# Splitting a block scatter in two and reordering every engine's queue in a recurrent attention kernel

## The chip, the cores and the metric
One core of one Trainium2 chip. The time is the device time of one execution in microseconds, as the median of three runs. The engines are PE (TensorE), DVE (VectorE), ACT (ScalarE), POOL (GpSimd) and SP (SyncE, which here only issues transfers). Each runs its own list of instructions in order and waits on semaphores for the others.

## The reference
Two layers on 1024 tokens (2 sequences of 512) of width 256. Layer 0 is causal softmax attention with 16 heads of 16 and a mixture of 8 experts of which each token uses 2. Layer 1 is a gated delta-rule recurrence, followed by 2 shared and 16 routed experts (2 per token). The recurrence is most of the time; per key head (16 of width 128, two value heads each) and token it does

```
Sk    = einsum("bhi,bhipj->bhpj", k_t, state)
delta = (v_t - Sk) * b_t
state = state * d_t + einsum("bhi,bhpj->bhipj", k_t, delta)
o     = einsum("bhi,bhipj->bhpj", q_t, state)
```

after a causal convolution of four taps over q, k and v, and before an RMS norm, a gate silu(z) and an output projection.

## The kernel before
The recurrence is cut into chunks of 128 tokens: 16 heads times 4 chunks give 64 units `u` (head h = u // 4, for both sequences and both value heads at once). Inside a unit the token-by-token rule becomes a triangular system. Its steps carry short names, by which the planner knows them:

- `row`, `dec`: the decay row is fetched (tile RC), POOL adds the bias and masks it, ACT takes the exponential.
- `gram`, `pt`: PE forms K K^T and Q K^T, DVE scales them into M and PTE. `pl`, `pm`, `py`: POOL splits M and adds the identity.
- `a` and `b`, once for each level: the ladder that inverts the unit triangular matrix by doubling. `a` is a PE product with a DVE copy (ZF, ZL), `b` a PE product with an ACT copy (XYLM). `r`, `c` finish the inverse (DVE tiles R and W).
- `KS`, `U`, `so`: the state step, which each unit hands to the next. `sq`, `on`, `ot`, `os`, `ol`, `y`, `yl`: norm (ACT, POOL), transpose (PE, with the gate on DVE), splitting (POOL) and output projection (PE).

Per head there are also the projections `ck`, `cq`, `cv` (PE), each with three convolution taps on DVE (`ck1` to `cv3`, line L2148), `kn` (norm of the keys), `Vt`, `Zt`. From head 2 on the first levels of the inverse are done for a whole head at once on DVE and POOL: LM is parked in DRAM (`ls`), its 16x16 diagonal blocks are gathered (`dg`, 8 transfers), inverted (`iv1`, `p8`, `iv2`, `q8`, `iv3`), copied by ACT (`xc`, tile XY) and scattered back into the parked array by `sx`: for each of 8 blocks and each of 2 matrices one transfer of 8 KB, 16 in a row on SP. Then `ld` loads each unit's matrices (XYLM).

Layer 1 also needs the routing of its 16 experts: `cnt` (PE, then DVE), `own`, `tiles` and `hits` are arithmetic on DVE alone (L1832 to L1891), `slot` a small product; after that POOL issues indirect transfers, `sw` for expert weights (L2745) and `sr` for token rows (L2729), and `sT`, `su`, `sd` run the tiles in 8 groups.

All of this is one list of parts with an engine, an assumed cost and predecessors. `Plan.arrange` places them one after another: of the ready parts it takes the one with the smallest begin time (plus an offset from the table LATER), in steps of 0.0517 us, and breaks ties by rank plus an offset from the table RANK. What comes out is the fixed order of each engine's instructions and the PSUM bank of each product. The engines then run those orders with semaphores. `cum` is the product that ends the preparation of the decays; `pre(4)` is the DVE step behind it. In what follows a part is named with its indices, such as `so(0,1)`, the state step of unit 0, second sequence.

Of the kernel before, what the change touches and what calls it, by code (L numbers as in the profile page):

```python
# [78 lines left out]
RANK = {  # L79
    "KS": {"ACT": 15.02}, "KS:first": {"ACT": 149.13, "DVE": 1181.68, "PE": 1010.25},  # L80
    "KS:last": {"ACT": -222, "DVE": -206.26, "PE": 190.34}, "U": {"ACT": -18.46, "PE": -931.18},
    "U:first": {"ACT": -151.06, "PE": 608.87}, "U:last": {"ACT": 335.37, "PE": -335.84}, "Vt": {"ACT": 90.31},
    "Vt:first": {"ACT": 3712.37, "PE": 1204.71}, "Zt": {"ACT": -129.73}, "Zt:first": {"ACT": 4.87},
    "a": {"DVE": -1349.82}, "a:first": {"DVE": 740.41, "PE": -888.94}, "a:last": {"DVE": 24.87, "PE": -779.69},
    "am:0": {"POOL": -60.05}, "am:1": {"POOL": 376.57}, "b": {"ACT": 1157.23},
    "b:first": {"ACT": -993.02, "PE": -2311.64}, "b:last": {"ACT": -395.1, "PE": -102.16},
    "c": {"DVE": -4239.84, "PE": -1258.51}, "c:first": {"DVE": -25.7, "PE": -55.9},
    "c:last": {"DVE": 213.97, "PE": -5.57}, "cb": {"DMA": 10.36, "DVE": -81.97, "POOL": -375.65},
    "cc": {"POOL": -343.13}, "ck": {"ACT": 922.98}, "ck1": {"DVE": 973.5}, "ck1:first": {"DVE": -591.14},
    "ck2": {"DVE": 768.74}, "ck2:first": {"DVE": 155.35}, "ck3": {"DVE": 253.77}, "ck3:first": {"DVE": 284.76},  # L90
    "ck:first": {"ACT": -349.27, "PE": -22.49}, "cnt": {"DVE": 580.25, "PE": -336.59}, "cq": {"ACT": -31.68},
# [10 lines left out]
    "fWV": {"POOL": 260.31, "SP": -44.28}, "fin": {"DVE": -134.8, "SP": -83.9}, "fld": {"SP": -358.28},
    "fs": {"ACT": 250.33}, "fst": {"SP": 132.24}, "fup": {"POOL": 169.77, "SP": -539.82},
    "fx": {"POOL": -199.89, "SP": -573.4}, "g0": {"ACT": 80.6}, "gg": {"DVE": -115.68, "PE": -29.2},
    "gram": {"DVE": 41.18, "PE": -508.06}, "gram:first": {"DVE": -141.6, "PE": -416.39},
    "gram:last": {"DVE": 154.44, "PE": -407.02}, "gt": {"ACT": 337.25, "PE": -330.13}, "hits": {"DVE": -209.58},
    "iv1": {"DVE": -424.93}, "iv2": {"DVE": -224.76}, "iv3": {"DVE": -443.76}, "kb": {"POOL": 171.24},
    "kb:first": {"POOL": 14.23}, "kn": {"ACT": 1374.77, "POOL": 134.84},
    "kn:first": {"ACT": 275.87, "PE": -156.91, "POOL": -308.37}, "kns": {"ACT": -780.5},
    "kns:first": {"ACT": -329.63}, "ld": {"DMA": -180.19, "SP": -410.02}, "ld:last": {"DMA": 45.92, "SP": 283.5},  # L110
    "ln1": {"ACT": -20.84, "DVE": 222.58, "PE": -88.46}, "ls": {"DMA": 81.69, "SP": -20.91},
    "ls:last": {"DMA": 56.89, "SP": 366.03}, "max": {"SP": 2.19}, "mk:0": {"POOL": 433.31}, "mk:1": {"POOL": 219.74},
    "nr2": {"DVE": -44.87}, "nrm": {"POOL": -113.07}, "oc:0": {"ACT": 189.5}, "oc:1": {"ACT": -379.67},
    "ol": {"POOL": -32.95}, "ol:first": {"POOL": -31.41}, "ol:last": {"POOL": 774.22}, "on": {"ACT": -904.27},
    "on:last": {"ACT": -566.16}, "op": {"DVE": 286.87, "PE": -1756.01}, "os": {"POOL": -177.43},
    "os:first": {"POOL": 81.33}, "os:last": {"POOL": -38.41}, "ot": {"DVE": -204.1, "PE": -586.61},
    "ot:first": {"DVE": -24.55, "PE": -145.69}, "ot:last": {"DVE": 322.85, "PE": -452.77},
    "ov:1": {"DVE": -366.86, "PE": 232.57}, "own": {"DVE": -429.99}, "p1:0": {"DVE": -68.36, "PE": -121.26},
    "p1:1": {"DVE": 27.26}, "p8": {"POOL": -213.19}, "pd": {"DMA": 325.19, "SP": -895.26},
    "pd:first": {"DMA": 175.96, "SP": 517}, "pd:last": {"DMA": 313.5, "SP": -493.56},  # L120
    "pf": {"DVE": 172.9, "SP": 243.4}, "pl": {"POOL": 6.37}, "pl:first": {"POOL": 15.59}, "pl:last": {"POOL": -36.33},
    "pm": {"POOL": 68.09}, "pm:first": {"POOL": 634.35}, "pm:last": {"POOL": 639.07},
    "pre": {"ACT": -830.11, "DVE": 94.48}, "ps": {"DMA": -177.84, "SP": 3.21},
    "ps:first": {"DMA": -267.15, "SP": -317.62}, "ps:last": {"DMA": 20.34, "SP": 735.5}, "pt:last": {"DVE": -311.51},
    "pv:0": {"PE": 8.46}, "pv:1": {"PE": -666.95}, "py": {"POOL": 1261.98}, "py:first": {"POOL": 206.17},
    "q8": {"POOL": 6.96}, "r": {"DVE": -581.63}, "r:first": {"DVE": -65.75, "PE": -1765.17},
    "r:last": {"DVE": -57.39, "PE": -1050.4}, "rb:0": {"SP": -298.18}, "rc:0": {"DVE": 1012.4},
    "rc:1": {"DVE": -121.62}, "rd:0": {"SP": 78.63}, "rd:1": {"SP": 210.21}, "row": {"DMA": -531.58},
    "row:first": {"DMA": -85.8, "SP": -250.3}, "row:last": {"DMA": 241.31, "SP": -1186.17}, "rt1": {"DVE": 298.72},
    "sT": {"ACT": -139.9, "PE": 3.29}, "sc:0": {"ACT": -400.63, "PE": 0.38}, "sc:1": {"ACT": 450.62, "PE": -125.1},  # L130
    "sd": {"DVE": 1296.02}, "slot": {"DVE": -98.48, "PE": -539.68}, "so": {"DVE": -153.94, "PE": -273.42},
    "so:first": {"DVE": 578.75, "PE": -1724.17}, "so:last": {"DVE": 0.93, "PE": -188.84}, "spg": {"POOL": -19.8},
    "sq": {"ACT": 298.13, "POOL": -483.87}, "sq:first": {"ACT": 126.75}, "sq:last": {"ACT": 593.63},
    "sr": {"POOL": -624.67}, "ss": {"SP": -5.07}, "stack": {"SP": -387.27}, "su": {"ACT": -324.78},
    "sw": {"DMA": 73.95, "POOL": 13.31}, "sx": {"DMA": -333.8, "SP": 100.24}, "tiles": {"DVE": 6.35},
    "tn": {"DVE": 265.94, "PE": -10.92}, "tn0": {"DVE": -15.3}, "top": {"ACT": -537.19, "DVE": 25.86},
# [4 lines left out]
    "yl:first": {"DVE": 1177.21, "PE": -193.29}, "yl:last": {"DVE": 19.32, "PE": 30.9},  # L141
}


LATER = {
    "KS": {"ACT": 0.21}, "KS:first": {"ACT": 0.05, "DVE": 0.02}, "KS:last": {"ACT": 0.16, "DVE": 0.43},
    "U:first": {"ACT": 0.06}, "U:last": {"PE": 0.25}, "Vt": {"ACT": 0.38}, "Vt:first": {"ACT": 0.21},
    "am:0": {"POOL": 0.76}, "am:1": {"POOL": 0.36}, "b:last": {"ACT": 0.25}, "c:last": {"PE": 0.14},
    "cb": {"DMA": 1.91, "DVE": 0.84}, "ck1:first": {"DVE": 0.07}, "ck3": {"DVE": 0.03}, "ck:first": {"ACT": 0.7},
# [2790 lines left out]
```

## Time and profile before
| | us |
|---|---|
| median of 3 runs | 1229.77 (1229.45 to 1232.14) |
| the profiled execution | 1230.72 |
| its span | 1228.9 |
| PE busy in the span | 1159.3 (94%) |
| DVE, POOL, ACT busy | 1047.5, 863.4, 841.6 |
| mean granted TensorE clock | 0.982 |

The profile shows one execution. A row of a view names a source line, an engine, an operation and its tiles, the count, the busy time and the idle time ahead of it with what ended that idle time. Line numbers are those of the kernel before.

### The profile page before, as it was taken

The page shows a single profiled execution, that of the slowest core. Times are in us where ns is not written, and L with a number is a line of the kernel's source. Part 1 is how long each engine was busy: PE and PEld are TensorE (multiplying, and loading weights), DVE is VectorE, ACT ScalarE, POOL GpSimd, SP SyncE. Part 2 cuts the span into 40 slices and gives each one's busy share as a digit, 9 for nine tenths or more (in the row PEclk, how much of TensorE's full clock was granted, in tenths as well). Part 3 has the DMA queues.
Part 4 walks back from the last instruction along what each step waited for, and adds up shares of the span by engine and source line. Part 5 has one row for each costly group of instructions (what it writes and reads, how often), then busy time and mean ns, then how long its engine had stood idle before and what let it go on. Part 6 is the DMA issues. An engine that isn't in the chain of part 4 may idle for free. (4 is left out here: it accounts for less than half of the span.)

```text
span 1228.9 us, 28718 instructions
## 1 busy us (share of the span) xinstructions
PE 1159.3 (94%) x9866; PEld 977.3 (80%) x9866; DVE 1047.5 (85%) x2365; ACT 841.6 (68%) x2396; POOL 863.4 (70%) x1101
## 2 busy tenths in 40 slices
PE   8898999888799899999999999999999999999997
PEld 7654566666698888989898988888888888888886
DVE  5796356899988989898988999899899889999988
ACT  4014643477487678877787778777877787787775
POOL 4115342839879888797969888787878787867634
PEclk9999999889799999999999999999999999999999
DMA  7942122214226556565636375655454663626331
GB/s 232 249 122 102 49 74 74 86 40 150 84 78 161 119 169 149 156 188 132 190 94 207 94 214 143 189 146 152 141 163 130 179 171 90 186 56 208 73 117 44
DMA packets 219492, 165.94 MB, mean 135 GB/s; under 512 B 103572, under 2 KB 186772, under 8 KB 219348
## 3 DMA queue, kind: packets, MB, share of 16 engines
q1 hardware_dynamic: 214612, 149.82, 44.0%
q0 software_dynamic: 4736, 14.29, 3.9%
q8 instruction: 79, 1.29, 0.4%
q14 instruction: 65, 0.53, 0.1%
HBM read 115.71 MB, written 48.16 MB: 133 GB/s over the span
## 5 line engine op out<-in xcount | busy, mean ns | idle before, releaser
L2556 ACT ACTIVATE XYLM<-ps 128x512 f16<-128x512 f32 x216 | 125.9, 598 | 54.1 <-PE ps L1647 53.1
L2148 DVE SCALAR_TENSOR_TENSOR KQ<-ps,cw,KQ 128x511 f32<-128x511 f32 (+2 forms) x192 | 140.6, 742 | 12.7 <-ACT KQ L2492 11.0
L2148 DVE SCALAR_TENSOR_TENSOR yv<-ps,cw,yv 128x511 f32<-128x511 f32 (+2 forms) x192 | 139.8, 741 | 8.6 <-ACT yv L2492 6.7
L1339 PE MATMUL ps<-XH,WVh 128*128 128x256 f32 (+1 forms) x384 | 133.5, 348 | 7.1 <-ACT KN L2507 4.5
L1339 PE MATMUL ps<-XH,WVl 128*128 128x256 f32 (+1 forms) x384 | 122.9, 320 | 0.0
L1339 PE MATMUL ps<-XL,WVh 128*128 128x256 f32 (+1 forms) x384 | 122.8, 320 | 0.0
L2590 ACT ACTIVATE sq<-O 128x128 bf16<-128x128 f32 x256 | 79.5, 310 | 28.7 <-DVE O L2328 14.5
L2596 ACT ACTIVATE O<-O,small 128x128 f32<-128x128 f32 x256 | 82.1, 400 | 14.2 <-POOL small L2834 14.0
L2278 DVE TENSOR_TENSOR ZL<-ps,cst 128x256 f16<-128x256 f32 x192 | 77.9, 415 | 10.4 <-PE ps L1633 8.9
L1339 PEld LDWEIGHTS ps<-XH,WVh 128*128 128x128 f32 x384 | 72.8, 190 | 12.8 <-ACT KN L2507 5.4
L2853 POOL TENSOR_TENSOR OGL<-O,OGH 128x512 fp32r<-128x512 f32 x62 | 80.6, 1300 | 2.8
L1704 PEld LDWEIGHTS ps<-De,PT 128*128 128x128 f32 x512 | 75.5, 193 | 5.7
L2786 POOL TENSOR_TENSOR RC<-RC,dec 128x512 f32<-128x512 f32 x64 | 67.2, 1051 | 17.0 <-DMA RC<-crow 16.8
L1704 PE MATMUL ps<-De,PT 128*128 128x128 f32 x512 | 77.8, 277 | 0.0
L1339 PEld LDWEIGHTS ps<-XH,WVl 128*128 128x128 f32 x384 | 72.5, 189 | 5.8
L1339 PEld LDWEIGHTS ps<-XL,WVh 128*128 128x128 f32 x384 | 72.9, 190 | 3.3
L2578 ACT ACTIVATE D<-ps,dec 128x128 f32<-128x128 f32 x192 | 60.9, 378 | 20.6 <-PE ps L1690 18.9
L2439 ACT ACTIVATE PT<-ps 128x1024 f32<-128x1024 f32 (+3 forms) x64 | 44.1, 705 | 43.8 <-PE ps L1436 41.8
L2834 POOL TENSOR_TENSOR small<-small 128x4 f32<-128x4 f32 (+1 forms) x66 | 67.4, 1021 | 5.5
L1737 PE MATMUL ps<-WOh,OGH 128*128 128x256 f32 x248 | 67.2, 304 | 2.9 <-DVE O L2347 2.9
L1612 PE MATMUL ps<-KQ 128*128 128x256 f32 x256 | 68.2, 389 | 0.2 <-ACT st L2604 0.2
L2565 ACT ACTIVATE QSc<-ps,dec 128x128 f32<-128x128 f32 x192 | 59.4, 377 | 13.1 <-DVE RH L2304 12.8
(359 smaller groups left out, 4083.0 us busy)
## 6 DMA issues: line engine op xcount, KB each, us to landing
XYLM<-parked SPq DMA_DIRECT2D x56, 512.0 KB, 5.3
RC<-crow SPq DMA_DIRECT2D x128, 128.0 KB, 4.7
decayed<-PTE SPq DMA_DIRECT2D x64, 256.0 KB, 3.4
PT<-decayed SPq DMA_DIRECT2D x64, 256.0 KB, 3.1
parked<-LM SPq DMA_DIRECT2D x56, 256.0 KB, 4.9
WV<-in_WV SPq DMA_DIRECT2D x16, 512.0 KB, 4.1
exr<-in_ex SPq DMA_DIRECT2D x16, 384.0 KB, 3.9
WK<-in_WK SPq DMA_DIRECT2D x16, 256.0 KB, 3.0
```

Of the source, the lines that this page charges most:

```text
L1339: m = pe.matmul(o, a, b, start=c + k == 0, stop=c == 1 and k == 2)
L1612: m = pe.matmul(ps[:, bk, 256 * b:256 * b + 256].rearrange("p (k t) -> p k t", k=2), K[:, h % 3, at], KQ[:, h % 3, :, at], start=True, sto ...
L1704: m = pe.matmul(ps[:, bk, 256 + 128 * v:384 + 128 * v], PT[:, u % 2, 2 * b + v, :], De[:, b, v, :], start=True, stop=True)
L1737: pe.matmul(ps[:, bk, 256 * b:256 * b + 256], OGH[:, 2 * b + v, :], weights[:, h % 2, v, :], start=v + k == 0, stop=False, skip_group_chec ...
L2148: m = dve.scalar_tensor_tensor(out=dst[:, k:512], in0=ps[:, bk, 0:512 - k], scalar=cw[:, h, j, 3 - k:4 - k], in1=dst[:, k:512], op0=ALU.mu ...
L2278: leave(dve.tensor_tensor(half(zl(k), k, 0), p, lv(k), ALU.mult), "a", u, k)
L2556: leave(act.activation(changed(u, k), ps[:, bank("b", u, k), :].rearrange("p (c n t) -> p c n t", c=2, t=1 << (k - 1)), ACT.Copy), "b", u, k)
L2590: act.activation(sq[:, 1, :], O[:, u % 2, l, :], ACT.Square, accum_out=so[:, u % 2, l:l + 1]).then_inc(s_sqo, 1)
L2596: m = act.activation(O[:, u % 2, l, :], O[:, u % 2, l, :], ACT.Copy, scale=ro[:, u % 2, l:l + 1])
L2786: pool.tensor_tensor(rc.rearrange("p (b v) t -> p b v t", b=2), rc.rearrange("p (b v) t -> p b v t", b=2), bias.unsqueeze(3).broadcast_to( ...
L2834: pool.tensor_tensor(ro[:, u % 2, four], ro[:, u % 2, four], mh[:, four], ALU.pow).then_inc(s_ro, 1)
L2853: pool.tensor_tensor(OGL[:], O[:, u % 2], OGH[:].bitcast(F32), ALU.subtract).then_inc(s_ogl, 1)
```

## The change
Three edits. The scatter of a head's inverted blocks becomes two parts, `sx` (first matrix, eight transfers) and `sy` (second matrix, eight transfers), which the planner may place apart; `ld` and the next head's `xc` wait for both. The rank of a part is rounded to six digits. And both tables, RANK and LATER, hold other numbers throughout, from a search that began with all offsets at zero, so that the order on every engine is another one. No computing instruction is added or removed, and the 224 transfers of the scatter stay 224.

```diff
 RANK = {
-    "KS": {"ACT": 15.02}, "KS:first": {"ACT": 149.13, "DVE": 1181.68, "PE": 1010.25},
...
+    "ck1": {"DVE": 691.8}, "ck1:first": {"DVE": 1.19}, "ck2": {"DVE": -983.47}, "ck2:first": {"DVE": 832.48},
...
-                                              rank + RANK.get(phase(label), {}).get(eng, 0.0), int(takes) if n == 0 else 0)
+                                              round(rank, 6) + RANK.get(phase(label), {}).get(eng, 0.0), int(takes) if n == 0 else 0)
...
-    P.add(("xc", h), rank + 0.2, ("ACT", 1.1, (("iv3", h), "DVE"), (("sx", h - 1), "DMA") if h > LEAD else None))
-    P.add(("sx", h), rank + 0.2, ("SP", 7.9, (("xc", h), "ACT")), ("DMA", 0.3))
+    P.add(("xc", h), rank + 0.2, ("ACT", 1.1, (("iv3", h), "DVE"), *((((k, h - 1), "DMA") for k in ("sx", "sy")) if h > LEAD else ())))
+    P.add(("sx", h), rank + 0.2, ("SP", 3.95, (("xc", h), "ACT")), ("DMA", 0.3))
+    P.add(("sy", h), rank + 0.2, ("SP", 3.95, (("xc", h), "ACT")), ("DMA", 0.3))
...
-                        for k in range(2):
-                            sp.dma_start(parked[h % 2, k, at, :, at].rearrange("r q c -> q r c"),
-                                         XY16[at, k, :].rearrange("q (r c) -> q r c", c=16)).then_inc(d_sx, 16)
+                        sp.dma_start(parked[h % 2, 0, at, :, at].rearrange("r q c -> q r c"),
+                                     XY16[at, 0, :].rearrange("q (r c) -> q r c", c=16)).then_inc(d_sx, 16)
+                elif what == "sy":
+                    w.wait_ge(d_l1, 128)
+                    w.wait_ge(s_xc, 2 * (h - LEAD + 1))
+                    for b in range(8):
+                        at = slice(16 * b, 16 * b + 16)
+                        sp.dma_start(parked[h % 2, 1, at, :, at].rearrange("r q c -> q r c"),
+                                     XY16[at, 1, :].rearrange("q (r c) -> q r c", c=16)).then_inc(d_sx, 16)
```

SP, the scatter of the third head that has one. Before, all 16 transfers stand in one row (the PT load, PTE and LM stores around it belong to other units):

```order
L1153 DMA WV<-in_WV 128x2x512
L1285 DMA parked<-XY 16x16x16 x16
L1299 DMA PT<-decayed 128x512
L1268 DMA parked<-LM 128x2x512
L1262 DMA decayed<-PTE 128x512 x2
```

After (its lines stand 1 to 7 further down):

```order
L1306 DMA PT<-decayed 128x512
L1285 DMA parked<-XY 16x16x16 x8
L1263 DMA decayed<-PTE 128x512
L1292 DMA parked<-XY 16x16x16 x8
L1306 DMA PT<-decayed 128x512
```

One store of PTE goes between the halves. This is so in 4 of the 14 heads; in the other 10 the halves stand back to back.

DVE, where the routing arithmetic ends and the first state step is made. Before (L1882 to L1891 are the end of `tiles` and `hits`, W is `c(0)`, the copies S and O are `so(0,0)` and `so(0,1)`, ZL a ladder step, line L2186 is `slot`):

```order
L2292 SCALAR_TENSOR_TENSOR W<-ps,XYLM 128x512
L1874 TENSOR_SCALAR small<-small 128x16
L1876 SCALAR_TENSOR_TENSOR st<-small,cst 128x512
L1880 TENSOR_REDUCE small<-st 128x16
L1882 SCALAR_TENSOR_TENSOR st<-cst,small 128x512
L1884 SCALAR_TENSOR_TENSOR small<-small 128x16
L1887 TENSOR_TENSOR st<-st,cst 128x512
L2278 TENSOR_TENSOR ZL<-ps,cst 128x8x32
L1891 SCALAR_TENSOR_TENSOR st<-cst,small 128x2048
L2278 TENSOR_TENSOR ZL<-ps,cst 128x4x64
L2324 COPY S<-ps 128x128 x2
L2330 COPY O<-ps 128x256
```

After, the end of the same work (yv are convolution taps, R is `r`, W is `c`, L1898 is the last long step of the routing; the earlier routing rows stand 26 to 47 rows ahead of it):

```order
L2155 SCALAR_TENSOR_TENSOR yv<-ps,cw,yv 128x511
L2285 TENSOR_TENSOR ZL<-ps,cst 128x4x64
L2155 SCALAR_TENSOR_TENSOR yv<-ps,cw,yv 128x510
L2285 TENSOR_TENSOR ZL<-ps,cst 128x8x32
L2155 SCALAR_TENSOR_TENSOR yv<-ps,cw,yv 128x509
L1898 SCALAR_TENSOR_TENSOR st<-cst,small 128x2048
L2285 TENSOR_TENSOR ZL<-ps,cst 128x4x64
L2291 SCALAR_TENSOR_TENSOR R<-ps,idk 128x512
L2299 SCALAR_TENSOR_TENSOR W<-ps,XYLM 128x512
L2291 SCALAR_TENSOR_TENSOR R<-ps,idk 128x512
L2299 SCALAR_TENSOR_TENSOR W<-ps,XYLM 128x512
L2193 CAST toki<-ps 128x32
```

W of unit 0 and the state step have moved behind all of the routing, and behind the taps of head 1 and the whole ladders of units 1 and 2.

POOL, near the output of units 2 to 4. Before (L2745 is `sw`, an indirect transfer of expert weights; RC is `dec`, LM `pl` and `pm`):

```order
L2745 DMA wt<-in_ud,rowi 128x512
L2786 TENSOR_TENSOR RC<-RC,dec 128x512
L2789 AFFINE_SELECT RC<-RC 128x512
L2806 CAST LM<-M 128x512
L2745 DMA wt<-in_ud,rowi 128x512
L2810 TENSOR_TENSOR LM<-M,LM 128x512
```

After (L2736 is `sr`, the indirect transfer of token rows):

```order
L2736 DMA st<-xnd,toki 128x256
L2832 TENSOR_TENSOR XYLM<-XYLM,cst 128x512
L2793 TENSOR_TENSOR RC<-RC,dec 128x512
L2796 AFFINE_SELECT RC<-RC 128x512
L2813 CAST LM<-M 128x512
L2736 DMA st<-xnd,toki 128x256
L2817 TENSOR_TENSOR LM<-M,LM 128x512
```

The row gathers of later groups have moved up: between `pm(3)` and `os(4)` POOL issues 16 indirect transfers where it issued 11.

## Rows read from the trace of the kernel before

**Rows 1.** The page, part 1: busy time by engine

```profile
PE 1159.3 (94%) x9866; PEld 977.3 (80%) x9866; DVE 1047.5 (85%) x2365; ACT 841.6 (68%) x2396; POOL 863.4 (70%) x1101
```

**Rows 2.** Windows: stretch and length, busy time by engine, granted clock, DMA, GB/s

```profile
215.00:258.00 43.00, 32.90 (x129) 24.48 (x128) 35.53 (x97) 23.83 (x55) 26.70 (x43) 0.80 0.20 62
258.00:321.00 63.00, 50.23 (x448) 41.79 (x447) 59.41 (x122) 41.74 (x91) 49.86 (x63) 0.90 0.37 108
310.00:330.00 20.00, 15.07 (x125) 12.49 (x126) 17.52 (x33) 8.31 (x25) 16.82 (x18) 0.70 0.24 79
300.00:500.00 200.00, 177.95 (x1729) 158.49 (x1728) 177.05 (x387) 139.05 (x404) 170.08 (x210) 0.95 0.50 133
500.00:1200.00 700.00, 687.90 (x6225) 614.35 (x6224) 631.78 (x1436) 546.05 (x1669) 548.35 (x691) 1.00 0.53 146
1200.00:1229.00 29.00, 22.27 (x166) 19.63 (x162) 24.46 (x60) 16.37 (x59) 14.82 (x23) 0.94 0.15 46
```

**Rows 3.** Waits of PE, 215 to 330 us: total, times, longest

```profile
PE ps L1690 <- DVE W L2292: 4.6, 1, 4.6
PE ps L1339 <- ACT KN L2507: 4.5, 1, 4.5
PE ps L1644 <- DVE ZL L2278: 2.6, 2, 2.3
```

**Rows 4.** Timeline of DVE, 300 to 320 us: start, duration, instruction

```profile
309.52 0.68 DVE L2292 SCALAR_TENSOR_TENSOR W<-ps,XYLM 128x512 f32<-128x512 f32 x1
...
314.84 3.96 DVE L1891 SCALAR_TENSOR_TENSOR st<-cst,small 128x2048 f16<-128x2048 f32 x1
```

**Rows 5.** Timeline of PE, 310 to 321 us and 397 us

```profile
310.34 2.04 PE L1690 MATMUL ps<-V,W 128*128 128x128 f32 x8 [4.58 <-DVE W L2292]
...
320.07 2.05 PE L1612 MATMUL ps<-KQ 128*128 128x256 f32 x4
...
397.16 1.03 PE L1612 MATMUL ps<-KQ 128*128 128x256 f32 x4
```

**Rows 6.** Groups of DVE instructions by form, 258 to 321 us

```profile
L2232 DVE SCALAR_TENSOR_TENSOR M<-ps,small,E 128x256 f32<-128x256 f32 x10 | 4.3, 476 | 0.3 <-PE ps L1612 0.3
L2148 DVE SCALAR_TENSOR_TENSOR yv<-ps,cw,yv 128x511 f32<-128x511 f32 x5 | 3.7, 743 | 1.2 <-ACT yv L2492 1.2
L2278 DVE TENSOR_TENSOR ZF<-ps,cst 128x256 f16<-128x256 f32 x9 | 3.6, 416 | 0.6 <-PE ps L1633 0.6
```

**Rows 7.** Groups of POOL instructions, 300 to 500 us

```profile
L2745 POOL DMA_INDIRECT wt<-in_ud,rowi x9 | 9.7, 1076 | 1.7 <-issue 1.3 <-DVE rowi L1864 0.3
L2729 POOL DMA_INDIRECT st<-xnd,toki x8 | 8.4, 1053 | 1.3 <-issue 1.3
```

**Rows 8.** Timeline of the SP queue from 1045 us

```profile
1045.22 8.99 SPq L1285 DMA_DIRECT2D parked<-XY  x16
1054.32 0.39 SPq L1268 DMA_DIRECT2D parked<-LM  x1
```

**Rows 9.** Waits of PE in the whole span

```profile
PE ps L1633 <- DMA XYLM<-parked: 1.3, 2, 1.0
PE ps L1737 <- DVE O L2347: 2.9, 1, 2.9
```

**Rows 10.** Timeline of PE: a step from f16 to f32 operands, 1176.9 us

```profile
1177.00 0.28 PE L1647 MATMUL ps<-XYLM,ZL 128*128 128x64 f16 x4
1177.11 0.36 PE L1737 MATMUL ps<-WOh,OGH 128*128 128x256 f32 x1
1177.32 0.28 PE L1737 MATMUL ps<-WOl,OGH 128*128 128x256 f32 x1
1177.43 0.29 PE L1737 MATMUL ps<-WOh,OGH 128*128 128x256 f32 x1
```

**Rows 11.** Timeline of POOL, end of the program

```profile
1218.04 0.75 POOL L2628 TENSOR_TENSOR OGL<-O,OGH 128x256 fp32r<-128x256 f32 x1
1218.88 0.25 POOL L2832 TENSOR_SCALAR small<-small 128x2 f32<-128x2 f32 x1
```

More of the change, by code:

```diff
@@ L85 @@
[L85 to L90, printed above, removed]
@@ L102 @@
[L102 to L106, printed above, removed]
@@ L107 @@
[L107 to L133, printed above, removed]
@@ L134 @@
[L134 to L136 removed]
[4 rows of a table removed]
[L141 removed]
+    "KS": {"ACT": 193.7, "DVE": -1159.55, "PE": -9.43}, "KS:first": {"ACT": -511.96, "DVE": -5.7, "PE": 478.58},
@@ new lines @@
+    "fup": {"POOL": 68.3, "SP": 328.89}, "fx": {"POOL": -337.8, "SP": 339.98}, "g0": {"ACT": 116.13},
+    "gg": {"DVE": 134.87, "PE": -836.23}, "gram": {"DVE": 499.88}, "gram:first": {"DVE": -143.08, "PE": -239.53},
+    "gram:last": {"DVE": 386.91, "PE": -0.95}, "gt": {"PE": -119.84}, "hits": {"DVE": -508.39},
+    "iv1": {"DVE": 464.58}, "iv2": {"DVE": 197.13}, "iv3": {"DVE": -113.73}, "kb": {"POOL": -2936.68},
+    "kb:first": {"POOL": 794.36}, "kn": {"ACT": 80.94, "PE": -1106.56, "POOL": -22.67},
@@ new lines @@
+    "ol": {"POOL": -1151.16}, "ol:first": {"POOL": 189.71}, "ol:last": {"POOL": 169.57}, "on": {"ACT": 126.05},
+    "on:first": {"ACT": -397.34}, "on:last": {"ACT": -354.81}, "op": {"DVE": -368.4, "PE": -101.03},
+    "os:first": {"POOL": -901.48}, "os:last": {"POOL": 692.34}, "ot": {"DVE": -319.7, "PE": 0.56},
+    "ot:first": {"DVE": -221.14, "PE": -409.83}, "ot:last": {"DVE": 3.64, "PE": 333.85},
+    "ov:1": {"DVE": 66.5, "PE": 6.49}, "own": {"DVE": 94.93}, "p1:0": {"DVE": -630.61, "PE": -259.22},
@@ new lines @@
+    "p1:1": {"DVE": -1091.25}, "p8": {"POOL": -554.27}, "pd": {"SP": 182.5},
+    "pd:first": {"DMA": 110.29, "SP": 172.75}, "pd:last": {"DMA": 139.21}, "pf": {"DVE": 29.04, "SP": 414.33},
+    "pl": {"POOL": -790.99}, "pl:first": {"POOL": -139.27}, "pl:last": {"POOL": 117.47}, "pm:first": {"POOL": 101.49},
+    "pm:last": {"POOL": 154.34}, "pre": {"ACT": -111.92, "DVE": -142.47}, "ps": {"DMA": -1342.78, "SP": -207.31},
+    "ps:first": {"DMA": 349.2, "SP": 248.72}, "ps:last": {"DMA": -769.74, "SP": 7.24}, "pt:first": {"DVE": -875.08},
@@ new lines @@
+    "pt:last": {"DVE": -36.48}, "pv:1": {"PE": -238.39}, "py": {"POOL": -179.66}, "py:first": {"POOL": -1182.23},
[3 rows of a table added]
+    "row:first": {"SP": 462.32}, "row:last": {"DMA": 1219.25, "SP": -289.47}, "rt1": {"DVE": 14.63},
+    "sT": {"ACT": 13.12, "PE": -1052.18}, "sc:0": {"ACT": 127.23}, "sc:1": {"PE": -241.49}, "sd": {"DVE": -58.76},
+    "slot": {"DVE": -507.58, "PE": -37}, "small": {"SP": -310.04}, "so": {"DVE": -516.33, "PE": -55.94},
+    "so:first": {"DVE": 103.85, "PE": 204.39}, "so:last": {"PE": 144.52}, "spg": {"POOL": -28.42},
@@ L142 @@
+    "yl:last": {"DVE": 50.6, "PE": -197.67},
 }
 LATER = {
[L146 to L149, printed above, removed]
-    "cnt": {"PE": 0.1}, "cq": {"ACT": 0.04}, "cq:first": {"PE": 0.01}, "crow": {"ACT": 1}, "cv": {"ACT": 0.02},
@@ L166 @@
[L166 to L170 removed]
+    "KS": {"ACT": 0.01}, "KS:first": {"DVE": 0.03, "PE": 0.03}, "KS:last": {"ACT": 0.36, "PE": 0.13},
@@ new lines @@
+    "U:first": {"ACT": 1.75}, "U:last": {"ACT": 0.24}, "Zt:first": {"ACT": 0.08, "PE": 0.02}, "a:last": {"DVE": 0.01},
+    "am:0": {"POOL": 0.42}, "am:1": {"POOL": 0.51}, "c:first": {"DVE": 1.22, "PE": 0.01}, "c:last": {"PE": 0.23},
+    "cb": {"DMA": 0.57, "DVE": 0.53}, "cc": {"POOL": 0.99}, "ck2:first": {"DVE": 1.23}, "ck3": {"DVE": 0.1},
+    "ck3:first": {"DVE": 0.02}, "ck:first": {"ACT": 0.65}, "cnt": {"PE": 0.01}, "cq1": {"DVE": 0.15},
+    "cq3:first": {"DVE": 0.08}, "crow": {"ACT": 0.25, "SP": 2.31}, "cv1:first": {"DVE": 0.03}, "cv2": {"DVE": 0.18},
@@ new lines @@
+    "cv3:first": {"DVE": 0.03}, "dd:0": {"SP": 0.81}, "dd:1": {"SP": 0.72}, "dec": {"ACT": 0.07},
+    "dec:first": {"ACT": 0.15, "POOL": 0.07}, "dec:last": {"ACT": 0.27, "POOL": 0.19}, "dg": {"SP": 1.12},
+    "dn": {"DVE": 0.01}, "exd:1": {"DVE": 0.7}, "exg:1": {"ACT": 0.42, "DVE": 0.01}, "fWK": {"POOL": 0.66, "SP": 0.2},
+    "fWO": {"SP": 0.91}, "fWV": {"SP": 0.6}, "fin": {"DVE": 2.38, "SP": 0.73}, "fld": {"SP": 1.72},
+    "fup": {"POOL": 0.06}, "fx": {"POOL": 0.2, "SP": 0.94}, "g0": {"ACT": 1.14}, "gg": {"DVE": 0.07},
@@ new lines @@
+    "pd:last": {"DMA": 0.24, "SP": 1.77}, "pf": {"DVE": 0.58}, "pm:last": {"POOL": 0.04}, "ps:first": {"DMA": 1.51},
+    "pt": {"DVE": 0.03}, "pt:last": {"DVE": 0.1}, "r": {"DVE": 0.02}, "r:first": {"PE": 0.08}, "rb:1": {"SP": 0.78},
+    "rc:0": {"DVE": 0.12}, "rc:1": {"DVE": 1.54}, "rd:0": {"SP": 0.22}, "rd:1": {"SP": 0.03}, "row": {"DMA": 0.02},
+    "row:first": {"DMA": 2.17, "SP": 1.19}, "row:last": {"SP": 0.16}, "rt1": {"DVE": 0.05}, "sc:0": {"ACT": 0.41},
+    "sc:1": {"ACT": 0.02}, "slot": {"PE": 1.23}, "small": {"SP": 1.11}, "so:first": {"DVE": 0.11},
```

67 lines of the change are left out of this document (36 added, 31 removed), and 24 rows, old and new, of the table RANK.

## The prediction
> **What bounds the kernel now.** I read the page first. PE is busy 94% of the span, 1159.3 of 1228.9 us [rows 1], and since the change leaves every matmul in place, the time can move only through PE's idle time (69.6 us), through the clock it is granted, and through small costs between neighbouring matmuls. The second view is the windows [rows 2]. Each row gives the busy time of PE, weight loads, DVE, ACT and POOL. Between 500 and 1200 us PE is idle for only 12.1 of 700 us, so no order can win much there. The idle time is in three places. From 215 to 258 us, where layer 0 hands over to layer 1, it is 10.1 us. From 258 to 321 us it is 12.8 us while DVE is busy 59.4 of 63 us: DVE bounds this stretch. From 300 to 500 us it is 22.0 us (some 10 of them before 321, so counted already), with DVE busy 177 and POOL 170 of 200 us. The last 29 us have 6.7 us. Third come the waits of PE [rows 3]: the longest is 4.6 us for W, the tile that ends the inverse of unit 0. The timelines show why: W is made at 309.52 us, between pieces of the routing arithmetic, and a 3.96 us routing step at 314.84 us lies ahead of a ladder step [rows 4]. PE pays twice, for after its wait of 4.58 us eight matmuls take 2.04 us, and four of another form take 2.05 us where they take 1.03 us later on [rows 5]; the granted clock was 0.70 of full speed from 310 to 330 us [rows 2], a mix of the 1.2 and 2.4 GHz levels, after PE had stood still.
>
> **The split scatter.** SP holds its queue for 8.99 us with the 16 transfers and then issues what has piled up, an LM store first [rows 8]. Split, each half holds about 4.5 us, and in 4 of 14 heads one PTE store leaves 4.5 us earlier; in the other ten nothing goes between. No instruction is added. PE waited for reloaded matrices for 1.3 us in the whole run [rows 9]. That bounds the gain at 1.3 us. The loss is bounded by the one store that now delays the second half: its issue is about 0.4 us, like the 0.39 us store [rows 8], in 4 heads, 1.6 us. Both ends are covered by the other queued units, so I take 0.
>
> **Hand-over, 215 to 258 us.** The two query projections (1.5 us each, as a projection takes in the chain of waits) that stood ahead of the attention output product now stand behind it, and two expert products stand ahead instead. PE's cover between the last expert product of layer 0 and the normalised rows becomes shorter by about 2.6 us, but DVE does three taps less in the chain (0.7 us each, 2.1 us), and POOL does the norm before a 3.5 us block of constants instead of behind. Together a wash: I take 0, with -1 to +2 us. The 4.5 us wait for ACT at KN [rows 3] stands behind a chain of table loads that is in both orders.
>
> **The DVE stretch, from `pre(4)` to `so(0,1)`.** Here the order changes most. Counting the parts on DVE between those two, the new order has nine more convolution taps, one more `gram` and `pt`, four more `a`, one more `x1`, two more `r` and one more `c`. With what an instruction takes start to start, a tap is 0.7 us (0.743 with its overlap), a pair of M or PTE 0.8 us, a ladder copy 0.33 us (0.416 with overlap) [rows 6], and R and W about 0.6 us (0.68 with overlap) [rows 4]: 6.3 + 1.6 + 1.3 + 0.3 + 1.2 + 0.6 = 11.3 us more DVE work ahead of `so(0,1)`. On PE the same stretch gains two `cv` and one `up` (1.5 us each), one `gram` (1.0 us, [rows 5]), one `kn` (0.5 us) and ladder products (3 `a`, 5 `b`, 2 `r`, 1 `c`, about 3 us) and loses two `dn` (1.7 us); with a small one about 7.4 us. The gap between what DVE must do and what PE has to do grows by 11.3 - 7.4 = 3.9 us, and in a stretch in which DVE is the bound, that is PE idle time. DVE was idle for 3.6 us of those 63 [rows 2], about 1 us of which the new order can fill. I take +3 us. The lower end is -6.2 (the first rival), the upper end is the full 11.3 us, if none of the PE work fits beside it. What comes behind is lighter: from `so(0,1)` to `so(3,1)` DVE has 9 us less to do and PE 5 us less, which ends the debt but doesn't pay it back, since PE's lost time isn't made up by a DVE that is ahead.
>
> **POOL, to `os(4)`.** Five more indirect transfers at 1.05 to 1.08 us [rows 7], one more `dec` and one more product of `q8` make about 9 us more POOL work between `pm(3)` and `os(4)`. The output product `y(4)` that waits for `os(4)` stands about 10 us of PE work later, measured from the end of layer 0, but part of that is the same DVE stretch. What is left is up to 5 us of lateness against PE, 3 of which the DVE delay already holds. Where such a chain ended late before, PE waited 2.9 us at L1737 [rows 9]. I take +1.5 us, between -1 and +6.
>
> **Fewer switches on PE.** Going from the f16 products of the ladder to f32 products costs: the first matmul runs 0.21 us to the next start, the following one 0.11 us [rows 10]. That is 0.1 us, of which the others of this kind show 0.08 to 0.09. The new order has 367 such steps where the old one had 388. 21 x 0.08 = -1.7 us, in a part of the program where PE is the bound. I keep 0 to -2.1 us.
>
> **Steady part and tail.** Between 500 and 1200 us every order leaves some waits; 12.1 us can become 8 or 18. At the end `os(61)` and `ol(61)` now come directly ahead of the last units' work on POOL, whose small norm step started the moment the split before it ended (1218.88 us, behind 0.75 us of splitting [rows 11]); that can push the last chain by up to 2 us. Against it the last residual additions have moved ahead of the chain. I take +0.5 us, between -4 and +6.
>
> **The sum.** Against the profiled execution (1230.7 us; its span is 1228.9): 0 + 0 + 3.0 + 1.5 - 1.7 + 0.5 = +3.3, which gives 1234.0. The median of the runs shown lies 0.95 us below the profiled execution, so I predict 1233.0 us.
>
> **A page against the trace.** The clock was at 0.70 from 310 to 330 us while PE was busy 15.07 us there [rows 2], so at full speed that work would have taken 4.5 us less. The Trainium skill (TensorE: Matmul & The Clock Gate, section Terms) prices such a loss as the time that the clock is held down times the share of pulses that are left out. By that rule 0.30 of 20 us, 6.0 us, are lost; the trace agrees with the mechanism, but the rule counts time in which PE had nothing to do. By the rule the first rival would be 1.5 us better than I say.
>
> **Rivals.** *Faster: the routing no longer stops the ladder.* In the old order PE stood still in whole blocks of 4.58 and 2.3 us and then ran at half clock [rows 3, 5]. In the new one, ladder copies and taps stand between the routing steps, and PE gets a little work all the time. If that keeps the clock up, the 4.5 us worked out above come back, the +3 and +1.5 vanish since PE's work counts at full speed, and with the switches the time is 1229.8 - 4.5 - 1.7 = 1223.6 us. For it: DVE's backlog was the same anyway, and the old order paid for it at the slow clock. Against it: between `cnt` and `c(0)` the new order has 24 us of DVE work beside 9 us of PE work, so PE idles as long, only in smaller pieces.
>
> *Much slower: POOL becomes the bound.* POOL was busy 170 of 200 us between 300 and 500 us [rows 2], and each of its steps has an idle gap around it. If the nine us that have moved up fall on the chain norm, split, output product, PE loses all of them beside the DVE term: 1229.8 + 3 + 9 - 1.7 = 1240 us. It decides where POOL's `os` is later than PE's arrival at `y`. For it: the 2.9 us wait [rows 9]. Against it: the outputs also stand later on PE. The Trainium skill (SBUF — State Buffer, section SBUF: two separate sides) says that POOL and a DVE instruction with two SBUF inputs take one port pair in turn and the loser waits for the whole instruction. No row here singles that out; by it, the more of POOL's work lies beside DVE's routing, the nearer this rival comes.
>
> *No change: the terms cancel.* The DVE delay and the waits that followed between 330 and 500 us overlap, since whatever PE waits for later has also gained 3 us. Then +3 - 1.5 (from the waits there) - 1.7 leaves 1229.6 us.
>
> *The split is what matters.* It would take the 1.3 us of waits for XYLM away: 1228.5 us, still within what can be told. The order shows that the halves are mostly not separated, so this is hardly a case of its own.
>
> **Chances.** The forecast, +2.5 to +8 us, 0.36; POOL as the bound 0.11; no change, with the split's case, 0.20; the routing rival and other gains 0.33. A measurement of this kernel can tell about 0.2%, 2.5 us, from no change. So faster 0.33, within 0.2% 0.20, slower 0.47. The range that holds 8 in 10 reaches from just below the first rival to a little past the POOL rival: 1220 to 1243 us. The forecast's own range is 1230 to 1238.
>
> **What would show it.** In the profile after: DVE busy over 95% from the decay preparation to the first state step, and S and O of unit 0 about 6 to 10 us later than 320 us; PE idle by 17 us or more between 258 and 330 us, where it was about 14; the clock below 0.9 there. If PE's idle time in that stretch is under 10 us and the clock stays at 1.00, the DVE term is wrong and the routing rival holds. POOL's wait at L1737 or L1712 over 3 us between 380 and 480 us would speak for the POOL rival. PE waiting for XYLM should stay under 2 us; if it falls to 0 and the time with it, the split counts for more than I say. If the time differs while idle time before 500 us does not, the term of the steady part is the one I have mis-sized.

## The result and the profile after
The changed kernel takes 1289.23 us (median of 4, 1281.6 to 1292.39) where the kernel before takes 1230.95 in the same session: ratio 1.0456, 95% interval 1.0421 to 1.0492. It is 4.6% slower. The prediction was 1233.0 us with a range of 1220 to 1243: wrong, by 56 us. The profiled execution took 1281.6 us, the shortest of the four; its span is 1279.9 us, 51.0 more than before, so the rows below account for 51 of the 58 us between the medians. Line numbers of the changed kernel lie 1 to 7 above those before.

Busy time by engine, after, against [rows 1]:

```profile
PE 1180.6 (92%) x9866; PEld 993.4 (78%) x9866; DVE 1059.6 (83%) x2365; ACT 838.9 (66%) x2395; POOL 864.7 (68%) x1101
```

The matmuls are the same 9866, yet PE is busy 21.3 us longer (1180.6 - 1159.3), and its idle time rose from 69.6 to 99.3 us, by 29.7. Together these are the 51.0 us. So two things grew: waits, and the time that the same work takes. The mean granted clock fell from 0.982 to 0.961. The windows after, against [rows 2] (the first two are the same stages, 11 us later: the hand-over to `cum`, and `cum` to `slot`):

```profile
226.00:269.00 43.00, 30.88 (x125) 22.07 (x124) 37.95 (x97) 22.25 (x45) 25.10 (x39) 0.84 0.19 62
269.00:342.00 73.00, 57.37 (x497) 47.11 (x496) 69.68 (x128) 44.11 (x102) 52.47 (x71) 0.82 0.31 96
300.00:500.00 200.00, 171.90 (x1634) 150.05 (x1633) 161.25 (x349) 127.72 (x348) 163.71 (x202) 0.90 0.43 119
500.00:1200.00 700.00, 672.56 (x5963) 601.47 (x5963) 625.10 (x1402) 523.59 (x1610) 551.38 (x695) 0.99 0.53 147
```

The row to look at is the last: 5963 matmuls where [rows 2] have 6225, and 27.4 us of PE idle time where there were 12.1, in the part in which I had said that no order can win much. The waits of PE over the whole span:

```profile
PE ps L1744 <- POOL OGH L2854: 12.4, 7, 4.8
PE ps L1719 <- ACT O L2603: 9.4, 6, 5.3
PE ps L1651 <- DVE ZL L2285: 7.4, 6, 3.8
...
PE ps L1752 <- POOL OGL L2860: 5.2, 4, 3.7
PE ps L1454 <- POOL PT L2692: 4.6, 3, 2.5
```

OGH and OGL are POOL's split of a unit's output (`os`, `ol`), for which the output projection waits: 17.6 us in all. Before, the only such wait was one of 0.2 us. POOL is not busier (864.7 against 863.4). What it waits for is this (before, then after; columns: total, times, longest):

```profile
POOL aT L2693 <- DMA rB<-inverses: 16.4, 7, 5.8
...
POOL wt L2755 <- DMA rows_out<-st: 4.2, 1, 4.2
POOL LM L2806 <- DMA parked<-LM: 3.3, 2, 1.9
...
POOL WO L2666 <- DMA WO<-in_WO: 0.8, 2, 0.4
```

```profile
POOL aT L2700 <- DMA rB<-inverses: 29.4, 7, 8.7
POOL WO L2673 <- DMA WO<-in_WO: 15.5, 6, 6.2
POOL st L2736 <- DMA rows_out<-st: 12.9, 4, 5.8
POOL LM L2813 <- DMA parked<-LM: 12.4, 5, 4.6
```

In these four kinds POOL waits 70.2 us for transfers to land where it waited 24.7; its other waits for transfers hardly changed in sum (96.7 before, 91.1 after). The 13 us more at `aT` lie in layer 0, ahead of any OGH. One case in full, from three timelines (SP's queue, POOL, PE):

```profile
871.58 1.14 SPq L1223 DMA_DIRECT2D rows_out<-st  x1
```

```profile
883.15 1.08 POOL L2736 DMA_INDIRECT st<-xnd,toki  x1 [5.80 <-DMA rows_out<-st]
884.26 1.05 POOL L2793 TENSOR_TENSOR RC<-RC,dec 128x512 f32<-128x512 f32 x1
885.47 0.65 POOL L2796 TENSOR_SCALAR_AFFINE_SELECT RC<-RC 128x512 f32<-128x512 f32 x1
886.26 0.96 POOL L2736 DMA_INDIRECT st<-xnd,toki  x1
887.23 0.62 POOL L2854 CAST OGH<-O 128x512 fp32r<-128x512 f32 x1
```

```profile
883.01 0.22 PE L1663 MATMUL ps<-XYLM 128*128 128x128 f16 x1
888.00 0.55 PE L1744 MATMUL ps<-WOh,OGH 128*128 128x256 f32 x1 [4.77 <-POOL OGH L2854]
888.35 0.42 PE L1744 MATMUL ps<-WOl,OGH 128*128 128x256 f32 x1
888.56 0.41 PE L1744 MATMUL ps<-WOh,OGH 128*128 128x256 f32 x1
```

The store of a routed group's rows is issued at 871.58 us and has landed at most 11.6 us later, when the gather that waits for it starts. The planner assumes 4.5 us for it (`ss`: 2.4 on SP and 2.1 behind). For the four stores of this kind for which a row gather waits, the time from issue to the gather's start is 4.9, 8.6, 10.5 and 11.6 us, so no single assumed number fits. The next group's first gather, `sr(28)`, stands in POOL's order where the planner thought the store had landed; POOL stops for 5.80 us, and the split of unit 33, which needs nothing of it, stands behind. PE waits 4.77 us and then starts a product every 0.21 us, where [rows 10] have 0.11 from the second product on: half the clock.

### The profile page after: what moved, and what is told of

The parts are those of the page before. It is cut to its first block and busy times, and to the rows that moved or that the text cites. A ratio compares the mean times of both kernels' runs of the same rounds, so it can differ in the third digit from the quotient of the medians.

```text
span 1279.9 us, 28750 instructions
## 1 busy us (share of the span) xinstructions
PE 1180.6 (92%) x9866; PEld 993.4 (78%) x9866; DVE 1059.6 (83%) x2365; ACT 838.9 (66%) x2395; POOL 864.7 (68%) x1101
## 5 line engine op out<-in xcount | busy, mean ns | idle before, releaser
L1346 PEld LDWEIGHTS ps<-XH,WVh 128*128 128x128 f32 x384 | 72.8, 190 | 11.3 <-DVE ZF L2285 4.6
L1744 PE MATMUL ps<-WOh,OGH 128*128 128x256 f32 x248 | 68.2, 306 | 12.5 <-POOL OGH L2854 12.4
L2793 POOL TENSOR_TENSOR RC<-RC,dec 128x512 f32<-128x512 f32 x64 | 67.4, 1052 | 11.6 <-DMA RC<-crow 11.3
L1619 PE MATMUL ps<-KQ 128*128 128x256 f32 x256 | 71.0, 401 | 0.0
L2817 POOL TENSOR_TENSOR LM<-M,LM 128x512 f16<-128x512 f32 x56 | 65.3, 1166 | 2.3
```

The lines of the kernel that those rows point to most:

```text
L1346: m = pe.matmul(o, a, b, start=c + k == 0, stop=c == 1 and k == 2)
L1619: m = pe.matmul(ps[:, bk, 256 * b:256 * b + 256].rearrange("p (k t) -> p k t", k=2), K[:, h % 3, at], KQ[:, h % 3, :, at], start=True, sto ...
L1744: pe.matmul(ps[:, bk, 256 * b:256 * b + 256], OGH[:, 2 * b + v, :], weights[:, h % 2, v, :], start=v + k == 0, stop=False, skip_group_chec ...
L2793: pool.tensor_tensor(rc.rearrange("p (b v) t -> p b v t", b=2), rc.rearrange("p (b v) t -> p b v t", b=2), bias.unsqueeze(3).broadcast_to( ...
```

## Experiments
All but two run orders fixed by hand: the planner's `arrange` was given a sequence in which to place the parts, so that an edit touches only what it names. Below, "old" and "new" are the placing sequences of the two kernels, both in the program with the split (in the old one the halves stand back to back). That this way of fixing an order costs nothing by itself is seen from the old one with a third buffer, further down: 1232.24 us. The texts set in ahead of each run name its theories by letters. Times are medians; the kernel before had 1231.4, 1231.3, 1231.7 and 1234.8 us in the four sessions.

**The split, undone.** In the changed kernel the halves are put back to back; every other engine stays.

```diff
+for _h in range(LEAD, HK):
+    SEQ.remove((("sy", _h), "SP"))
+    SEQ.insert(SEQ.index((("sx", _h), "SP")) + 1, (("sy", _h), "SP"))
```

> The changed kernel, with the two halves of each head's scatter put back to back again on SP (16 transfers in a row in all 14 heads); every other engine's order and every PSUM bank stay those of the changed kernel. Theory A (the new order of the engines' queues costs the time, the split costs nothing): 1284 to 1294 us, as the changed kernel. Rival B (the split itself costs: what stands between the halves delays the second half, the loads that need both come late): 1230 to 1240 us.

1296.67 us, ratio 1.0517 (1.0491 to 1.0543). Nothing comes back, so B, by which the split itself costs the time, falls. Whether the 7 us over the changed kernel come from putting the halves together is not shown: the two intervals touch, and of the 16.2 us between the two profiled executions 5.4 were there at `cum` (273.4 us against 268.0), almost 300 us ahead of the first place where the two orders differ. In the changed kernel the store between the halves was ready, and the second half began 0.5 to 0.8 us after the end of the first.

**The split alone, in the old order.** One transfer between the halves in 13 of 14 heads (in the last the load of a unit's matrices would have stood there, so the halves stay together):

```diff
+    OLD.remove((("sy", _h), "SP"))
+    _at = next(n for n in range(OLD.index((("sx", _h), "SP")) + 1, len(OLD)) if OLD[n][1] == "SP")
+    if OLD[_at][0][0] != "ld":
+        OLD.insert(_at + 1, (("sy", _h), "SP"))
...
```

> The kernel before in every engine's order and every PSUM bank, with the scatter alone split: in 13 of 14 heads the one transfer that stood behind the 16 (3 LM stores, 8 PT loads, 2 weight loads) now stands between the halves. Theory A (the split costs and gains nothing that can be measured): 1229 to 1233 us. Rival B (delaying the second half delays the loads behind it): 1236 us or more. Rival B' (what leaves 4.5 us earlier was waited for): 1226 us or less.

1250.44 us, ratio 1.0144 (1.0118 to 1.0171): a split with a transfer between the halves costs 19 us here, so B holds in this order. With the halves back to back and a third LM buffer the old order takes 1232.24 us (below), so it is the transfer between that costs, not the two parts. SP's queue, in this run and in the kernel before:

```profile
701.19 4.28 SPq L1414 DMA_DIRECT2D parked<-XY  x8
708.31 0.38 SPq L1398 DMA_DIRECT2D parked<-LM  x1
708.73 5.45 SPq L1421 DMA_DIRECT2D parked<-XY  x8
```

```profile
699.68 8.03 SPq L1285 DMA_DIRECT2D parked<-XY  x16
707.81 1.72 SPq L1268 DMA_DIRECT2D parked<-LM  x1
```

The LM store wasn't ready at 705.5 us, and SP stood with eight ready transfers behind it. In seven heads the second half begins 2.3 to 3.6 us after the end of the first, and the scatter of the last head comes 23 us later than before (1181.3 against 1158.7). PE's idle time between 500 and 1200 us is 24.9 us where [rows 2] have 12.1. My bound of 1.6 us counted the transfer's issue, not its wait. So the split was harmless where the transfer between was ready, and not where it wasn't.

**Empty tables.**

```diff
-RANK = {
...
+RANK = {}
+LATER = {}
```

> The changed program with both tables empty, so that the planner's own rules set the whole order. Theory A in the form that the search which began at zero fitted the tables to assumed costs and not to the chip: an order without tables runs about as long as the changed kernel or longer, 1285 to 1310 us. Rival C (the new tables do active harm, the bare planner's order is sound): 1240 to 1265 us.

1290.53 us (1.0448 to 1.0498): as slow as the changed kernel. The search from zero gained nothing that shows over no tables at all, and C, by which the planner's own order is sound, falls. The waits are not the same ones, though: here PE waited 12.2 us for PT and 11.9 us for XYLM from DRAM.

**Old tables on the new program.**

> The changed program (scatter in two parts, rounded ranks) with the two tables of the kernel before. The planner then no longer makes the old order: a part more and other ties shift what comes behind. Theory M (tables fit one program only, any other program with them is as good as unsearched): 1245 to 1270 us. Rival N (the old tables were good in themselves): 1228 to 1238 us.

1251.47 us (1.0131 to 1.0234), 20 us lost, so N falls: the old tables are not good by themselves. M is not shown, for a rival stands beside it. In this order too transfers stand between the halves, and in five of the 14 heads the second half begins 2.3 to 4.2 us after the end of the first, as in the run above that lost 19 us by that alone. How much the tables lose beyond it, no run tells.

**Where in time: old and new order exchanged at one point.** The runs differ in which order leads (FRONT), which follows (REST), and the part at which they are exchanged:

```diff
-ORDER1, BANKS1 = plan1().arrange()
+_front = set(FRONT[:FRONT.index((("cum",), "PE"))])
+ORDER1, BANKS1 = plan1().arrange(replay=[x for x in FRONT if x in _front] + [x for x in REST if x not in _front])
```

> The changed program with the order of the kernel before up to the product cum (the end of layer 0's work) and the changed kernel's order for all parts that are left. Theory A, losses add up stage by stage (11 us of the 51 us of longer span are there at cum): 1274 to 1282 us. Rival D (the late start of layer 1 and the lower clock there set everything that follows; with an old front the rest runs as before): 1230 to 1240 us.

> The mirror image: the changed kernel's order up to cum, the order of the kernel before for all that is left. Theory A: the 11 us of layer 0 and nothing else, 1238 to 1246 us. Rival D: 1275 us or more.

> The order of the kernel before up to the product c(4) (about 364 us), the changed kernel's order for all that is left. With the old order only up to cum the time was 1274.5. Theory A (losses add up by stage): the stretch from cum to c(4) was worth 11 to 14 us, the steady part the rest, so 1256 to 1264 us. Rival G (the stretch with the routing is where layer 1's loss is made, what comes later repays itself): 1240 us or less. Rival H (all of it in the steady part): 1272 us or more.

> The changed kernel's order up to the product slot (the end of the routing arithmetic), the order of the kernel before for what is left. With the new order up to cum the time was 1252.2. Theory A: the stretch from cum to slot adds 8 to 12 us, 1260 to 1265 us. My predicted term for this stretch was +3 us: 1254 to 1256 us.

> The changed kernel's order up to tn(1) (the end of the row maxima, 125 to 131 us), the old order behind it. With the new order up to cum the time was 1252.2. The row maxima ended 5 to 6 us late there and cum 11 to 17 us. Theory A (stages add up): 1237 to 1241 us. Rival K (the whole front loss is made in the rows behind tn(1)): 1233 us or less. Rival L (all of it ahead of tn(1)): 1248 us or more.

| order | us | ratio (95%) |
|---|---|---|
| new to `tn(1)`, old behind | 1240.89 | 1.0053 to 1.0106 |
| new to `cum`, old behind | 1252.25 | 1.0157 to 1.0213 |
| new to `slot`, old behind | 1252.93 | 1.0122 to 1.0190 |
| old to `cum`, new behind | 1274.46 | 1.0321 to 1.0377 |
| old to `c(4)`, new behind | 1275.38 | 1.0304 to 1.0400 |

Stages add up roughly (A, and H for the stretch up to `c(4)`), and D, by which the late start of layer 1 sets all that follows, falls. Up to `tn(1)` the new order costs 9 us (1240.9 - 1231.7), from there to `cum` 11, from `cum` to `slot` 1, behind `c(4)` 44 (1275.4 - 1231.3). The sum, 65, is 7 over the 58 measured. I can't place those 7, but the new front alone varies by more: with it `cum` came at 268.0 to 277.7 us in six profiles, and the changed kernel's is the earliest of them. The old front had 254.2 to 260.8 us in six. Each interval of the table is 3 to 6 us to either side, so a stage of a few us can't be told from none. G and my "11 to 14" us for the stretch from `cum` to `c(4)` were wrong: both exchanges there moved the time by 1 us or less.

**POOL's queue cleared.** In the changed kernel, POOL alone:

```diff
+behind("POOL", ("ol", 10), ("pl", 18), ("pm", 18), ("pl", 19), ("pm", 19))
+behind("POOL", ("ol", 17), ("sr", 16))
+behind("POOL", ("ol", 21), ("sr", 20))
+behind("POOL", ("ol", 29), ("pl", 38), ("pm", 38))
+behind("POOL", ("ol", 33), ("sr", 28), ("sr", 29))
```

> The changed kernel with five edits to POOL's order alone: pl(18), pm(18), pl(19), pm(19) behind ol(10); sr(16) behind ol(17); sr(20) behind ol(21); pl(38), pm(38) behind ol(29); sr(28), sr(29) behind ol(33). These are the places at which POOL stood waiting for a transfer to land (2.8 to 5.8 us) with a split os or ol queued behind it, and PE then waited 2.9, 1.7, 3.7, 2.0 and 4.8 us for that split, 15.1 us in all. Theory E (a POOL step that waits for a transfer, queued ahead of the split, holds up PE): the waits go and with them the slow products behind each, the time falls by 12 to 20 us to 1269 to 1277. Rival F (other chains are as late, or the moved steps are late for someone else): within 5 us of the changed kernel, 1284 to 1294.

1269.45 us, ratio 1.0293 (1.0259 to 1.0327): 20 us back. The waits of PE for these tiles in this run, and its window:

```profile
PE ps L1784 <- POOL OGH L2894: 1.4, 3, 1.0
PE ps L1792 <- POOL OGL L2900: 0.8, 2, 0.6
```

```profile
500.00:1200.00 700.00, 681.15 (x6081) 609.66 (x6081) 636.10 (x1433) 535.42 (x1651) 561.21 (x706) 1.00 0.55 148
```

17.6 us of waits are 2.2, the clock of that window is 1.00 instead of 0.99, and 118 more matmuls fit. From `cum` on, the profiled execution is 17.3 us shorter than the changed kernel's. E is shown, for 20 of the 58 us.

**The same with the old order up to `c(4)`, and a sixth edit** (`+behind("POOL", ("sq", 7), ("fWO", 2))`).

> The order of the kernel before up to c(4), the changed kernel's order behind it (1275.4 us so far), with the five POOL edits of the earlier run and a sixth: fWO(2), whose weights landed 7 us after their issue while POOL stood 6.2 us and PE then 5.3 us, behind sq(7). Theory E: the five edits are worth 20 us as they were in the changed kernel, the sixth 5 to 8 us: 1247 to 1252 us. Rival F (with another front, the same places no longer matter; the gain was luck of alignment): 1265 us or more.

1252.53 us (1.0133 to 1.0232), 22.9 less than without, half a us past the expected range. So the gain doesn't hang on one front, and F falls. The sixth edit is worth 3 us where I expected 5 to 8: in place of the load of WO, `pl(16)` then stood 5.5 us for the LM store, and PE's wait of 5.3 us shrank to 2.7 only.

**A third LM buffer.** It takes one of those waits away in any order. (To make room the zero tile shares the memory of another tile; that part of the edit is not shown here.)

```diff
-        LM = sb("LM", [128, 2, 2, 512], F16)
+        LM = sb("LM", [128, 3, 2, 512], F16)
...
-                    if u >= OWN + 2:
-                        w.wait_ge(d_ls[u % 2], 16 * ((u - 2 - OWN) // 2 + 1))
+                    if u >= OWN + 3:
+                        w.wait_ge(d_ls[u % 3], 16 * ((u - 3 - OWN) // 3 + 1) + 32 * (u % 3 == 2))
```

> The changed kernel's order on every engine, with a third LM buffer (the zero tile shares hT's memory to make room), so that pl(u) waits for the store of unit u-3 and not of u-2. Nothing is reordered and no transfer is added. POOL stood 12.4 us for that store in four places; PE gaps of 2.9, 2.0 and 1.5 us lay behind three of them. Theory E (POOL's queue held by a landing): these go with the slow products behind them, 1280 to 1285 us. Rival F (the next thing in the queue waits as long): 1287 to 1293 us.

> The order of the kernel before on every engine (halves of the scatter back to back), with the third LM buffer. Theory E: POOL's waits for that store (a few us in all) had no PE wait behind them in the old order, so nothing changes: 1229 to 1234 us. Rival O (a third buffer helps any order): 1226 us or less, a version faster than both kernels.

New order: 1281.18 us (1.0336 to 1.0448), where E put it, but the interval overlaps that of the changed kernel, so this run alone shows little. Its trace shows more: no wait of POOL for the LM store is left, and PE's waits for OGH fell from 12.4 to 7.0 us:

```profile
PE ps L1769 <- POOL OGH L2880: 7.0, 4, 4.3
...
PE ps L1777 <- POOL OGL L2886: 2.8, 2, 2.6
```

Old order: 1232.24 us, ratio 0.9986 (0.9963 to 1.0008), no change, as E says of an order that has slack there. This run is also the control for all the others: old order, program with the split, halves back to back, old time.

**Three products of layer 0 moved back**, in the order that is new up to `cum`.

```diff
+delay(SEQ, (("pv", 0, 1, 1), "PE"), (("p1", 1, 5, 0), "PE"))
+delay(SEQ, (("pv", 0, 1, 0), "PE"), (("sc", 0, 1, 2, 1), "PE"))
+delay(SEQ, (("pv", 0, 0, 3), "PE"), (("p1", 1, 4, 2), "PE"))
```

> The changed kernel's order up to cum, the old one behind it (1252.2 us so far), with three products of layer 0's attention on PE moved back: pv(0,0,3) behind p1(1,4,2), pv(0,1,0) behind sc(0,1,2,1), pv(0,1,1) behind p1(1,5,0). At the first two PE waited 1.3 and 0.9 us for POOL's mask, and then ran some 10 us at half the clock. Theory I (two short waits close together set off the slow clock, which costs more than they do): both go, 5 to 8 us less, 1244 to 1248 us. Rival J (the clock falls in this stretch whatever the order, since PE is as busy as DVE lets it be): 1250 to 1256 us.

1245.87 us (1.0090 to 1.0205), 6.4 less, in the expected range, but with an interval that holds both. Of the 9.6 us between the two profiled executions 2.6 were there at `cum` (270.9 us against 273.5), and the rest came behind it, where the orders are the same; so the 6.4 us can't be put down to the edit. What the edit is about, from the changed kernel's PE:

```profile
101.73 0.43 PE L1454 MATMUL ps<-PT,V 128*32 128x128 f32 x8 [1.27 <-POOL PT L2692]
...
104.34 1.94 PE L1454 MATMUL ps<-PT,V 128*32 128x512 f32 x8 [0.89 <-POOL PT L2692]
```

and its windows (clock in the third column from the right):

```profile
100.00:104.00 4.00, 2.18 (x27) 1.08 (x25) 2.05 (x4) 2.45 (x4) 3.67 (x6) 1.00 0.33 100
104.00:108.00 4.00, 3.66 (x22) 1.40 (x26) 0.95 (x2) 1.01 (x3) 3.83 (x6) 0.50 0.02 2
108.00:112.00 4.00, 4.00 (x22) 2.13 (x14) 1.31 (x3) 1.18 (x3) 1.84 (x3) 0.50 0.04 6
```

After the edit both waits are gone, and two of 0.7 us for DVE stand in the same place; the clock falls all the same, but is back at 0.91 from 108 to 112 us, where the same order without the edit still had 0.50:

```profile
104.00:108.00 4.00, 4.00 (x24) 1.89 (x21) 0.42 (x1) 0.77 (x2) 2.50 (x4) 0.50 0.14 47
108.00:112.00 4.00, 3.91 (x39) 1.94 (x38) 1.69 (x4) 2.27 (x3) 1.80 (x3) 0.91 0.05 21
```

(From 60 to 200 us the mean clock is 0.96 to 1.00 in the kernel before and five other profiles with the old front, and 0.88 to 0.95 in six with the new one.) Neither I nor J is settled.

**All repairs on the changed kernel.**

> The changed kernel with all repairs at once: the six POOL edits, the third LM buffer and the three pv products of layer 0 moved back. If the repairs add up as measured one by one (20 for five POOL edits, 3 for the sixth, 6 for the pv products, up to 5 for the buffer, from 1289): 1254 to 1262 us. Rival P (other faults of the order take their place): 1265 us or more.

1259.10 us (1.0149 to 1.0240), 30 us back; 24 are left over the kernel before in its session. One by one they had given 20, 3, 6 and 8 us, of which the last two were within the noise; the sum, 37, is a little more than the 30. PE's waits for OGH and OGL are 2.8 us. What is left stays open: it is spread over small waits and the front of the program, most of which no repair touches. No order tried here is faster than the kernel before.

## Why the prediction was wrong
- **The bound.** Held: time moved only through PE's idle time and clock. But I read the 12.1 us of idle time in the steady part as "no order can win much there" and forgot that an order can lose there.
- **The steady part, +0.5 us (-4 to +6).** This is the step that failed: it cost 44 us behind `c(4)` (1275.4 - 1231.3). "12.1 us can become 8 or 18" had no row behind it. They became 27.4 within 500 to 1200 us, the rest being slower products and the stretch to 500 us. I compared orders by the amount of work ahead of a part. What cost 20 of these 44 us was something else: parts that wait for a landing stood on POOL ahead of a split that doesn't (1289.2 to 1269.5 us when five groups of them were moved). Where the other 21 to 24 come from is open. The order I showed on POOL, with row gathers moved up, was the sign, and I priced it by the gathers' 1.05 us [rows 7].
- **Hand-over, 0 (-1 to +2), and all before it.** This failed too. The new order costs 21 us up to `cum` (1252.3 - 1231.4; 11.3 us in the profiled execution), 9 of them ahead of `tn(1)`, for which I had no term at all. The 4.5 us wait at KN, behind a chain that I said is in both orders, is gone, and waits of 3.9 us for XL and 3.8 us for hT have come. Which waits made the loss is open; `aT` waiting 13 us more for the reciprocals' round trip, and the clock rows above, are candidates, not shown.
- **The DVE stretch, +3 us.** Most signs came: DVE busy 69.68 of 73 us (95%), the clock at 0.82, W of unit 0 at 338.18 us and S at 343.69, 13 us later than before against `cum` (I had said 6 to 10). PE's idle time from 258 to 330 us came to 16.4 us, just under the 17 I had named. The price didn't show: exchanging this stretch costs 0.7 us (1252.25 to 1252.93), with 3 to 4 us of interval to either side of each, so 3 us can't be excluded, but 11 can. PE had done more by its end (497 matmuls where [rows 2] have 448 in 63 us); that this paid the delay back is my reading, not shown.

```profile
334.38 2.94 DVE L1898 SCALAR_TENSOR_TENSOR st<-cst,small 128x2048 f16<-128x2048 f32 x1
...
338.18 0.68 DVE L2299 SCALAR_TENSOR_TENSOR W<-ps,XYLM 128x512 f32<-128x512 f32 x1
...
343.69 0.49 DVE L2331 COPY S<-ps 128x128 f32<-128x128 f32 x2 [1.17 <-PE ps L1711]
```

- **POOL, +1.5 us, and the rival "POOL becomes the bound" (1240).** The place was right, `os` late for `y`, the cause wrong: POOL isn't short of time (864.7 us busy against 863.4), it stands still. The sign I had named, a wait of over 3 us between 380 and 480 us, came: 5.3 us at L1719 at 466.95 us, behind a stop of POOL of 6.17 us for the load of WO. And the 2.9 us wait that I took as a sign for this rival was for DVE's O, not for POOL [rows 9].
- **Switches on PE, -1.7 us.** Not tested alone, and too small to see beside 21.3 us of busy time gained by the slow clock.
- **The split, 0.** Nothing speaks against it for this change, but by luck: the transfer between was ready, a condition that I hadn't given. The bound of 1.6 us was wrong in kind, as the 19 us of the old order show.

## What to carry to other kernels
When a search sets the order of in-order queues, compare the planner's assumed landing of every kind of transfer with the issue and the waiter's start in a trace, and keep what waits for a landing behind what others wait for. Don't judge a new order by work ahead of a part or by the idle time that the old one has; look also, queue by queue, for waiting steps ahead of a part that the critical engine needs. And measure anew when tables fitted to one program are used on another: here one more part in the program went with 20 us, even if the runs don't say how much of that is the tables'.
